# One chip, one core: a three-part network, in which the last passes hand one of three sums of each query group to VectorE

## The reference

```python
x = x + conv_attention(group_norm(x))      # 8 heads, softmax over 768 keys of the same batch, two relative biases, causal in t
t = tokens(x)
n = layer_norm(t)                          # additive attention
q, k, v = n @ Wq.T, n @ Wk.T, n @ Wv.T
A = q @ W1[:, :128].T + b1                 # (16, 768, 16)
B = k @ W1[:, 128:].T
logits = einsum('bijh,h->bij', tanh(A[:, :, None] + B[:, None, :]), w2) + b2
t = t + softmax(logits) @ v
n = layer_norm(t)                          # mixture of experts
probs = softmax(n @ gate_w.T)              # 8 experts, the best 2 of each token, capacity 1920 rows
h = gelu(expert_in @ w1 + b1); expert_out = h @ w2 + b2
t = t + sum of the two gathered expert rows, weighted
```

## Time and profile before

| | |
|---|---|
| median of 3 runs | 2287.06 us (2283.81 to 2290.32) |
| the profiled execution | 2273.98 us, span 2272.2 us |
| mean granted TensorE clock in it | 0.972 of full speed |
| busy: PE, DVE, ACT, POOL | 2061.4 (91%), 1550.8 (68%), 1676.9 (74%), 1565.4 (69%) us |
| instructions | 54398 |

### The profile page before, as it was taken

One profiled execution on the slowest core, in us unless ns is written; L12 is line 12 of the kernel. 1 busy time (PEld: TensorE's weight loads), 2 busy tenths in 40 slices (PEclk: granted clock), 3 DMA queues, 4 the chain that ended last, 5 costly groups with the idle time before them and its releaser, 6 DMA issues.

```text
span 2272.2 us, 54398 instructions
## 1 busy us (share of the span) xinstructions
PE 2061.4 (91%) x19525; PEld 1206.4 (53%) x19525; DVE 1550.8 (68%) x4147; ACT 1676.9 (74%) x1934; POOL 1565.4 (69%) x1951
## 2 busy tenths in 40 slices
PE   4899999999999999999999999999999977899996
PEld 2555555555555555555555455555554433357775
DVE  7787777777777777777787778787867454324343
ACT  3549888888888888887888788888888978424332
POOL 5127677676767777776767676767677888547777
PEclk8899999999999999999999999999999999899998
DMA  4746413232222222222222322222221000025553
GB/s 120 109 87 149 89 35 78 44 72 47 67 46 65 51 69 47 73 49 72 50 71 51 71 50 64 54 62 52 58 44 26 12 6 5 24 56 87 84 89 34
DMA packets 157428, 137.41 MB, mean 60 GB/s; under 512 B 24665, under 2 KB 149814, under 8 KB 157104
## 3 DMA queue, kind: packets, MB, share of 16 engines
q1 hardware_dynamic: 119376, 109.87, 23.4%
q0 software_dynamic: 23824, 16.85, 5.4%
q10 hardware_dynamic: 13968, 7.30, 1.3%
HBM read 82.68 MB, written 54.52 MB: 60 GB/s over the span
## 4 chain that ended last, share of the span: by engine, by line
PE 26%; POOL 19%; issue 17%; DVE 15%; POOLq 13%; DVEq 5%; ACT 3%; DMA 2%; SPq 0%; ACTq 0%
POOL hidden L833 14%; POOLq L832 10%; PE logits L1035 7%; POOL out_dram L588 4%; DVE max_halves L1307 3%; PE av_bank L1021 3%; PE ring L1113 2%; PE scores L1005 2%; PE scores L1008 2%; PE ring L1135 2%; ACT hidden L954 1%; PE ring L1104 1%; ACT hidden L960 1%; PE ring L1127 1%; DVEq L1389 1%
## 5 line engine op out<-in xcount | busy, mean ns | idle before, releaser
L833 POOL TENSOR_SCALAR hidden<-b_rep,a_cols 128x768 f32<-128x768 f32 x1152 | 1054.7, 919 | 403.1 <-issue 234.8
L954 ACT ACTIVATE hidden<-hidden 128x2304 f32<-128x2304 f32 x384 | 816.9, 2127 | 66.2 <-POOL hidden L833 66.0
L1035 PE MATMUL logits<-hidden,w_shifted 128*32 128x384 f32 x6144 | 582.8, 497 | 61.0 <-ACT hidden L960 29.9
L1307 DVE TENSOR_REDUCE max_halves<-ring 128x4 f32<-128x512 f32 (+1 forms) x704 | 450.7, 659 | 158.9 <-PE ring L1113 158.2
L931 ACT ACTIVATE probs<-scores 128x512 f32<-128x512 f32 (+1 forms) x768 | 391.3, 547 | 196.9 <-PE scores L1008 190.9
L960 ACT ACTIVATE hidden<-b_rep,a_cols 128x768 f32<-128x768 f32 x384 | 358.6, 934 | 0.0
L1035 PEld LDWEIGHTS logits<-hidden,w_shifted 128*32 128x32 f32 x6144 | 163.9, 110 | 294.2 <-issue 233.6
L1113 PE MATMUL ring<-k_max,q_max 112*128 112x128 bf16 x2688 | 270.6, 223 | 13.8 <-DVE max_halves L1307 8.8
L1005 PE MATMUL scores<-bias_q,onehot_k 112*128 112x512 bf16 (+1 forms) x768 | 274.3, 358 | 3.7 <-DMA q_parts<-max_parts 2.1
L1008 PE MATMUL scores<-q_parts,k_parts 98*128 98x256 bf16 (+1 forms) x1536 | 275.6, 260 | 0.0
L1113 PEld LDWEIGHTS ring<-k_max,q_max 112*128 112x128 bf16 x2688 | 181.1, 99 | 154.8 <-issue 58.2
(11 more groups left out here) (272 smaller groups left out, 2618.7 us busy)
## 6 DMA issues: line engine op xcount, KB each, us to landing
qk_parts<-qk_parts_sb SPq DMA_DIRECT2D x16, 1152.0 KB, 4.3
q_parts<-qk_parts SPq DMA_DIRECT2D x192, 96.0 KB, 3.2
k_parts<-qk_parts SPq DMA_DIRECT2D x192, 96.0 KB, 4.3
q_max<-qk_parts SPq DMA_DIRECT2D x96, 96.0 KB, 3.0
k_max<-qk_parts SPq DMA_DIRECT2D x96, 96.0 KB, 3.6
expert_rows<-clear_row ACTq DMA_DIRECT2D x9, 792.0 KB, 5.1
x_in<-in_x_dram SPq DMA_DIRECT2D x96, 64.0 KB
x<-in_x_dram SPq DMA_DIRECT2D x96, 64.0 KB
```

Source lines behind the costliest of these rows:

```text
L833: last = g.tensor_scalar(hidden[:, q % SLOTS, o, :], b_rep[:, side], 1.0, a_cols[:, side, a_col(q, o):a_col(q, o) + 1], ALU.mult, ALU.add)
L954: s.activation(hidden[:, t % SLOTS, 0:3, :], hidden[:, t % SLOTS, 0:3, :], ACT.Tanh)
L1035: last = mm(logits[32 * g:32 * g + 32, half, 0:HALF], w2_shifted[:, k, :], hidden[:, q % SLOTS, g, HALF * half:HALF * half + HALF], start= ...
L1307: v.tensor_reduce(max_halves[:, h % 4:h % 4 + n_, BLOCK_PAIRS.index((qb, kb))], bank[:, 0:n_ * P].rearrange("p (h k) -> p h k", h=n_), AX. ...
```

## The change

Four parts.

- **Third sums.** `third_sum_moves(b, q)` holds for query groups 14 to 23 of batch 14 and 2 to 23 of batch 15. GpSimd makes two sums there, and VectorE the third, two ticks ahead, at the start of slot 3 of tick q-2. ScalarE waits for both.
- **Newton.** The conditions for who runs the Newton steps of norm 1 change: GpSimd where the pass has `mid` or `add`, VectorE where it has neither.
- **First expert chunk.** `down(0)` and `weigh(0)` come right behind `up(0)`, ahead of `up(1)`.
- **Fillers.** 20 filler products ahead of the experts, behind a wait for the last row that was sent.

```diff
+LAST = 15
+def third_sum_moves(b, q):
+    return b == LAST and q >= 2 or b == LAST - 1 and q >= 14
 # TensorE, experts
             def body(pair, e0, last_pair):
                 if not positive(e0):
+                    pe.wait_ge(rows_sent, 112 + 192 * NB)
+                    for _ in range(20):
+                        mm(scores[:, 0, :], ones_bf[0:112, :], bias_q[:, 0, 0:512], start=True, stop=True)
                     transpose_rows(pair, e0, 0)
                 for n in range(2 * CHUNKS):
 ...
                     up(pair, e0, n)
-                    if n or positive(e0):
+                    if n == 0 and not positive(e0):
+                        down(e0, 0)
+                    if n > 1 or positive(e0):
                         down(e0, n - 1)
 # VectorE, experts: the same for weigh
 # GpSimd
-                for o in range(3):
-                    if o == 2 or TICKS - SEND_FROM < q <= SEND_FROM:
+                n_ = 2 if third_sum_moves(b, q) else 3
+                for o in range(n_):
+                    if o == n_ - 1 or TICKS - SEND_FROM < q <= SEND_FROM:
                         pool.drain()
 ...
-                    if t == SCALE_AT[1] and (ps.has("mid") or ps.has("end")):
+                    if t == SCALE_AT[1] and (ps.has("mid") or ps.has("add")):
                         norm_scale(1, ps.batch("pre") - 2)
 # ScalarE
                         act.wait_ge(sums_ready, b * 24 + (t + 1))
+                        if third_sum_moves(b, t):
+                            act.wait_ge(third_ready, t - 13 if b < LAST else t + 9)
 # VectorE
+            def third_sum(ps, q):
+                b, side = ps.batch("add"), ps.side("add")
+                dve.wait_ge(logits_added, b * 24 + (q - SLOTS + 1))
+                v.tensor_scalar(hidden[:, q % SLOTS, 2, :], b_rep[:, side], a_cols[:, side, a_col(q, 2):a_col(q, 2) + 1],
+                                None, ALU.add).then_inc(third_ready, 1)
 ...
+                        if slot == 3 and ps.has("add") and t + 2 < TICKS and third_sum_moves(ps.batch("add"), t + 2):
+                            third_sum(ps, t + 2)
 ...
-                        if (ps.has("mid") or ps.has("end")) and t == 4 and slot == 3:
+                        if (ps.has("mid") or ps.has("add")) and t == 4 and slot == 3:
                             norm_seed(1)
-                        elif ps.has("pre") and not ps.has("mid") and (t, slot) in NORM_AT:
+                        elif not ps.has("mid") and not ps.has("add") and (t, slot) in NORM_AT:
                             norm_step(1, NORM_AT.index((t, slot)))
 ...
                                 if slot == 2:
-                                    dve.wait_ge(norm_scaled[1], ps.batch("pre") - 1)
+                                    dve.drain()
+                                    if ps.has("add"):
+                                        dve.wait_ge(norm_scaled[1], ps.batch("pre") - 1)
```

More of the change, by code:

```diff
@@ L342, in hybrid_kernel @@
         sums_ready = sem("sums_ready")
+        third_ready = sem("third_ready")
         tanh_done = sem("tanh_done")
@@ L564, in body @@
                         copy_rows(e0, n + 1)
-                    if n or positive(e0):
+                    if n == 0 and not positive(e0):
+                        weigh(pair, e0, 0)
+                    if n > 1 or positive(e0):
                         weigh(pair, e0, n - 1)
```

## The result

The changed kernel takes 2269.95 us (median of 8 runs, 2266.05 to 2278.11). The kernel before, run beside it, took 2287.33 us (8 runs). The ratio of the means is 0.9931, 95% interval 0.9911 to 0.9951, so 15.8 us less (11.2 to 20.4; the medians are 17.4 apart). The forecast was 14.2 less, 2272.9. The sum came out; two of its terms did not, and a term that it lacked made up for about half of what they fell short.

A forecast was written before the change was run, and what follows sets the result against it. The prediction took a chain walking GpSimd to bound the kernel, read place by place. 8.6 + 3.1 + 2.8 + 2.4 - 2.7 = 14.2 us less: 2259.8 profiled, 2272.9 median; 8-in-10 range 2265.5 to 2282.

The forecast's parts named there:

- Pass 14: Queries 14 to 23 give third sums to VectorE, closing the gap before pass 15's query 0: 2.3 us less, bounds 0 and 4.
- Pass 15, to query 7: Queries 2 to 6 without GpSimd's third sum, 3.64 a query: 2.6 us less; query 7 needs two drained sums: 1.1 less.
- Queries 7 to 23: Rest of pass 15: ScalarE sets the pace, 53.2 us plus 1.5 of stalls instead of 57.26: 2.6 us less.
- The stalls behind VectorE's queue: Pass 15 from query 7: third sums standing behind VectorE's copy of `probs1T` make ScalarE wait 1.5 us, bounds 0 and 4.
- rival C: Half-clock TensorE delays third sums, ScalarE stops 2.2 us in each of 5 blocks: 2.6 us slower, 2289.7; chance 0.08.
- Newton: Pass 16, Newton on VectorE: seed to `rows` 2.4 us instead of 5.56, gain 3.1, bounds 2.5 and 3.2.
- TensorE's clock in pass 16: Shorter idle keeps TensorE's full clock for fillers, gate and position products: 2.8 us less, bounds 0 and 2.8.
- Experts: Fillers keep 2.4 GHz, first scatter 3.6 us earlier, second chunk and GpSimd's stream 2.4: gain 2.4, bounds -2.1 and 3.6.
- a short gap in the scatters: Experts: second chunk's down products still stand behind the third chunk's first layer, so it comes only 2.4 us earlier.
- Head: Pass with only the maxima: eleven extra Newton instructions in VectorE's full stretch lose 2.7 us, bounds 0 and 3.0.
- the forecast's 8.6 for the third sums: Passes 14 and 15: all gains from third sums moved to VectorE, 8.6 us less.
- rival A: Shared port (0.2 gained a query, not 0.5) and VectorE's queue eat the sums, clock falls: 6.7 less, 2280.4; chance 0.27.

The follow-up runs named there:

- the changed kernel's repeat: The changed kernel run once more, with no edit, for its profile: 2273.77 us.
- the repeat: At the profile windows, the changed kernel run again unedited (2273.77 us); at the stop that cost 8 us, the kernel before run again unedited (2287.91 us).
- the two-source form: The changed kernel with VectorE's third sum written as scalar_tensor_tensor, reading two operands from SBUF: ratio to the kernel before 0.9968.

## Why the prediction was right, step by step

- **Pass 14** (2.3 forecast): 2.1 by the means. Right.
- **Pass 15, to query 7** (2.6 + 1.1): 4.2. Right, by the forecast's mechanism: GpSimd's pitch from query 2 to 6 is 3.60, 3.64 forecast (3.54 to 3.60 in eight of the nine profiles, 4.09 in one). The pitch before was 4.16 in the profile of the forecast and 4.36 to 4.38 in the other two, so the gain is a little larger than forecast.
- **Queries 7 to 23** (2.6): wrong in size, 0.0 by the means. The stalls behind VectorE's queue, 1.5 in the forecast, are what was too small. In the changed kernel's first profile and in the kernel with third sums alone (51.5 and 52.0), the 2.6 is there; ScalarE waits 0.9 and 1.1 us in all for third sums. In the six others it waits 2.5 to 3.5. The forecast had this stretch at 51.7 (54.3 - 2.6), with 1.5 of stalls in it; the mean of 54.4 makes some 4 of them. In the changed kernel's repeat the longest of these waits is rival C's mechanism, in one block of five. ScalarE there:

```profile
1919.30 2.12 ACT L971 ACTIVATE hidden<-hidden 128x2304 f32<-128x2304 f32 x1 [2.89 <-DVE hidden L1419]
...
1939.09 0.90 ACT L953 ACTIVATE probs<-logits,logit_bias 128x768 f32<-128x768 f32 x1 [1.98 <-DVE logit_bias L1520]
```

  TensorE before the first of these waits and in the same stretch of the first profile (the columns are busy time of PE, its weight loads, VectorE, ScalarE and GpSimd, then the granted clock): half clock for part of it, transposes late, and the third sum of query 12 stands behind the copy that waits for them. Windows of the repeat, then of the first:

```profile
1905.00:1919.00 14.00, 11.66 (x83) 4.64 (x75) 7.29 (x19) 11.41 (x11) 8.00 (x9) 0.76 0.00 1
```

```profile
1905.00:1919.00 14.00, 11.57 (x116) 5.55 (x120) 10.53 (x32) 13.40 (x14) 7.93 (x9) 1.00 0.03 7
```

  That the clock is behind the waits of the other profiles too is not shown: over queries 7 to 23 the granted clock is 0.97 in the kernel with third sums alone (52.0), and 0.97 also in two with 54.3 and 54.8.
- **Not in the forecast: the stop.** 1.6 to 2.7 us gained, as the third sums let GpSimd's row of sends end 6.5 instead of 9.3 us behind the last tanh product. The forecast priced GpSimd's freed time at nothing behind query 7; this is what it bought. This figure compares with the two profiles without third sums that have the stop; beside the third, which has none, nothing is gained, and how often the kernel before runs without it is not known.
- **Newton** (3.1): 3.1. From the maximum to the seed it is 0.4 longer by the means (8.8 before, 9.3), in six of ten profiles with a gap of 0.43 before the seed for which no releaser is named.
- **TensorE's clock in pass 16** (2.8): 2.9 in eight of ten profiles, 1.4 in two.
- **Experts** (2.4): 1.3. The cause was half wrong: fillers 2.3, the early second layer -1.0. The forecast called it "a short gap in the scatters" and still gave the layer a gain; the gap swallows all of it, and ScalarE's 0.77 is added.
- **Head** (-2.7): -2.8 at the first score product. That it reaches the end is not shown: the ratio is 0.9935 without these steps and 0.9931 with them.

Sum of the means: 2.1 + 4.2 + 0 + 2 + 3.1 - 0.4 + 2.6 (the clock over ten profiles) + 1.3 - 2.8 = 12.1, inside the 11.2 to 20.4 timed. The 3.7 us between it and 15.8 are in no place that was measured, and may be noise. That 14.2 lies nearer to 15.8 than the sum of the measured places does is luck: of the forecast's 8.6 for the third sums 6.3 are there, 1.1 of the experts' 2.4 is missing, and the stop, which was not in the sum, brings 2. That the difference could be carried over to the median unchanged was luck as well, since it was made on an execution without the stop. Of rival A the queue came as priced, 2.6 less behind query 7 against 2.1; its port (0.2 instead of 0.5 gained a query) shows in one profile of nine, and the clock fell in two of ten. The loss to the queue is about the size of the stop's gain.

## What to carry to other kernels

Before a sum is made from one profiled execution 13 us under the median, ask which stretch of it was lucky; here a stop that cost 8 us in the repeat was missing from it, and with it a gain of the change. When an engine is relieved, follow what it does next: of the late third sums more seems to have come through the sends behind them than through the sums. Work pulled forward at the head of a stream helps only as far as the second item comes forward too; look at the second scatter, not the first.

## What the runs showed of the hardware

- A row of back to back indirect DMAs on GpSimd (0.97 us each, 0.30 apart) that reached across the end of pass 15 came with a stop of VectorE in ten of eleven profiles: an instruction whose inputs had been ready for 2 to 7 us started only 1.65 to 1.9 us behind the end of the last DMA. It is no stop for the whole row: two copies start during it in the changed kernel (1948.94 and 1950.40 in its first profile), and with the two-source form four instructions run from 1965.21 on, 1.3 us before the last DMA ends, before VectorE stops again. In five of the ten TensorE has waits of 0.5 to 0.9 us without a releaser in the same time. With the row ended at 2.9 us behind the last tanh product there was no stop (two profiles). What holds the engines is not shown: one execution, the first of the kernel before, ran through the same row without it.
- VectorE and GpSimd on SBUF lengthen each other in a one-source and in a two-source form alike, in one meeting by up to about the whole length of the other's instruction; a VectorE instruction of 0.17 took 1.34 beside copies of 1.45.
- The head starts its maxima anywhere from 52.1 to 57.5 us with the same instructions ahead of them. In the kernel before, VectorE's last cast took 0.56 in one profile, with GpSimd's copies from 54.29 on, and 1.83 in the other, with the copies from 51.86 on.
